# Attention kernel, one core: turning a group's blocks before scaling a context, and a later second copy of the values

## The reference

```python
q, k, v = (proj(Wq, bq), proj(Wk, bk), proj(Wv, bv))
scores = jnp.einsum('bhqd,bhkd->bhqk', q, k) * SCALE
mask = (adj_matrix + bond_matrix)[:, None, :, :]      # both are adj
scores = scores * mask
attn = jax.nn.softmax(scores, axis=-1)
ctx = jnp.einsum('bhqk,bhkd->bhqd', attn, v)
ctx = ctx.transpose(0, 2, 1, 3).reshape(b, seq_len, EMBED_DIM)
return jnp.einsum('bse,fe->bsf', ctx, Wo) + bo
```

## Time and profile before

| | |
|---|---|
| median of 3 runs | 418.44 us (414.08 to 418.67) |
| the profiled execution | 418.86 us, its span 416.3 us |
| mean granted clock of TensorE | 0.989 |
| PE busy | 92% |
| DVE busy | 93% |
| ACT busy | 87% |
| POOL busy | 60% |
| DMA | 222 GB/s on average |

### The profile page before, as it was taken

One profiled execution on the slowest core, in us unless ns is written; L12 is line 12 of the kernel. 1 busy time (PEld: TensorE's weight loads), 2 busy tenths in 40 slices (PEclk: granted clock), 3 DMA queues, 4 the chain that ended last, 5 costly groups with the idle time before them and its releaser, 6 DMA issues.

```text
span 416.3 us, 12182 instructions
## 1 busy us (share of the span) xinstructions
PE 382.1 (92%) x3628; PEld 291.4 (70%) x3628; DVE 386.2 (93%) x1592; ACT 361.6 (87%) x1223; POOL 249.6 (60%) x379
## 2 busy tenths in 40 slices
PE   8989999999996999999999999899999999997772
PEld 6766777777674877777777776677777777675542
DVE  4988999999997799999999999999999999999865
ACT  4699999989897798999999999889899999999560
POOL 3143557677573775748577575757758474555455
PEclk9999999999999899999999999999999999999898
DMA  8468889989988789889989888888999898888632
GB/s 272 131 173 238 236 201 254 245 237 247 244 237 234 191 223 244 244 243 251 253 237 246 241 237 235 230 242 233 248 245 248 227 232 208 219 234 183 144 105 76
DMA packets 65427, 92.29 MB, mean 222 GB/s; under 512 B 8529, under 2 KB 48722, under 8 KB 65362
## 3 DMA queue, kind: packets, MB, share of 16 engines
q1 hardware_dynamic: 47426, 66.35, 63.9%
q10 hardware_dynamic: 17936, 25.17, 18.0%
HBM read 26.22 MB, written 8.39 MB: 83 GB/s over the span
## 4 chain that ended last, share of the span: by engine, by line
DVE 33%; PE 28%; DMA 12%; SPq 11%; issue 9%; ACT 4%; POOL 1%; DVEq 0%; ACTq 0%; POOLq 0%
DVE boxes L540 15%; DVE probs L521 13%; SPq L208 9%; DMA v_boxed<-v 8%; PE ctx_bank L404 7%; PE out_bank L421 5%; PE proj_bank L333 5%; PE out_bank L351 4%; PE row_bank L264 3%; ACT probs L728 3%; DMA carried<-boxes 3%; PE turn_bank L281 2%; SPq L217 2%; DVE stats L567 1%; DVE low_top L530 1%
## 5 line engine op out<-in xcount | busy, mean ns | idle before, releaser
L728 ACT ACTIVATE probs<-probs,low_top 128x256 f32<-128x256 f32 x512 | 254.6, 504 | 12.1 <-DVE low_top L530 12.1
L521 DVE CUSTOM_DVE_ANT_0 probs<-row_bank,adj_rows 128x256 f32<-128x256 f32 x512 | 187.4, 414 | 6.7 <-PE row_bank L264 5.9
L540 DVE STREAM_TRANSPOSE boxes<-probs 128x1536 f32<-128x1536 f32 x62 | 109.6, 1768 | 0.0
L333 PE MATMUL proj_bank<-xt_parts,w_parts 128*128 128x512 f32 x360 | 99.2, 411 | 0.0
L728 ACT ACTIVATION_READ_ACCUMULATOR probs<-probs,low_top 128x1 f32 x512 | 99.1, 194 | 0.0
L333 PEld LDWEIGHTS proj_bank<-xt_parts,w_parts 128*128 128x128 f32 x360 | 62.9, 188 | 30.5 <-issue 19.9
L404 PE MATMUL ctx_bank<-carried,v_boxed 128*32 128x256 f32 x744 | 61.9, 392 | 18.3 <-DMA v_boxed<-v 12.2
L867 POOL COPY wide<-shares 128x512 f32<-128x512 f32 x32 | 19.5, 610 | 92.2 <-DVE shares L548 92.2
L264 PE MATMUL row_bank<-kq 32*128 32x256 f32 x1024 | 73.3, 400 | 0.5 <-DVE top L521 0.5
L404 PEld LDWEIGHTS ctx_bank<-carried,v_boxed 128*32 128x32 f32 x744 | 32.3, 111 | 43.4 <-issue 31.4
L264 PEld LDWEIGHTS row_bank<-kq 32*128 32x128 f32 x1024 | 46.3, 184 | 11.7 <-issue 6.4
(11 more groups left out here) (85 smaller groups left out, 461.1 us busy)
## 6 DMA issues: line engine op xcount, KB each, us to landing
carried<-boxes SPq DMA_DIRECT2D x248, 192.0 KB, 3.9
xt<-in_x_t SPq DMA_DIRECT2D x32, 256.0 KB, 3.5
adj_rows<-in_adj ACTq DMA_DIRECT2D x32, 256.0 KB, 4.8
xr<-in_x ACTq DMA_DIRECT2D x32, 256.0 KB, 3.8
v_boxed<-v SPq DMA_DIRECT2D x124, 64.0 KB, 3.0
out<-result ACTq DMA_DIRECT2D x31, 256.0 KB, 5.3
w_whole<-in_wk ACTq DMA_DIRECT2D x2, 128.0 KB, 3.7
w_whole<-in_wq SPq DMA_DIRECT2D x1, 256.0 KB, 4.3
```

What stands on the lines that cost most here:

```text
L333: last = nc.tensor.matmul(proj_bank[:], w_parts[:, a, which, t, c * P:(c + 1) * P], xt_parts[:, pair % 2, b, t, :], start=(half_ == 0 and ...
L521: last = nc.vector.tensor_tensor_reduce(probs[:, h % RING, t * S:(t + 1) * S], row_bank[j][:, t * S:(t + 1) * S], adj_rows[:, (g // 2) % 2 ...
L540: nc.vector.transpose(boxes[:, n % BOXES].rearrange("p a h (f q) -> p (h f) a q", q=D), probs[:, first:first + BOXED, :].rearrange("p h (f ...
L728: last = nc.scalar.activation(tile, tile, ACT.Exp, bias=low_top[:, g % 2, J * c + j, t:t + 1], accum_out=sums[:, g % 2, t, j * T + c:j * T ...
```

## The change

In DVE's `step(g)` the first box now stands ahead of `scale_context(g - 2)` and not behind it. In SP's `step(g)` `carry_v(g + 1)` now stands last, behind `carry_boxes(2g)`. Since the values' copies are now issued later, they are counted on four semaphores in place of two. Everything else, on all engines, stays as it was; no instruction is added or taken away.

```diff
-        stored, v_in = ([sem(f"{name}{n}") for n in range(2)] for name in ("stored", "v_in"))
-
-        x_in, adj_in, carried_in = ([sem(f"{name}{n}") for n in range(4)] for name in ("x_in", "adj_in", "carried_in"))
+        stored = [sem(f"stored{n}") for n in range(2)]
+
+        x_in, adj_in, v_in, carried_in = (
+            [sem(f"{name}{n}") for n in range(4)] for name in ("x_in", "adj_in", "v_in", "carried_in"))
...
-                                 ).then_inc(v_in[n % 2], 16)
+                                 ).then_inc(v_in[n % 4], 16)
...
                 if 0 < g <= LAST:
                     carry_boxes(2 * g - 1)
-                if 0 <= g + 1 < LAST:
-                    carry_v(g + 1)
                 if g > 0 and is_pair((g + 1) // 2 + 3):
                     load_x_t((g + 1) // 2 + 3, (g + 1) % 2)
                 if 0 <= g < LAST:
                     carry_boxes(2 * g)
+                if 0 <= g + 1 < LAST:
+                    carry_v(g + 1)
...
-                    pe.wait_ge(v_in[g % 2], 64 * (g // 2 + 1))
+                    pe.wait_ge(v_in[g % 4], 64 * (g // 4 + 1))
...
+                if is_group(2 * g - 1):
+                    box(2 * g - 1)
                 if 0 <= g - 2 < LAST:
                     scale_context(g - 2)
-                if is_group(2 * g - 1):
-                    box(2 * g - 1)
```

## The result

The changed kernel takes 436.0 us in the median of 6 runs (432.59 to 440.31), the kernel before 417.96 us (414.08 to 418.92): a ratio of 1.042, with a 95% interval of 1.036 to 1.049. It is slower, as forecast, and by about 18 us where 10 were forecast; the time lies on the upper edge of the range, 424 to 436. The profiled execution took 437.35 us with a span of 435.1 us, 18.8 more than before.

What follows compares the result with a forecast made beforehand. DVE's floor of 11.65 us and a two-step loop bound steps at 11.90; 26 steps at 12.33 plus 27.7 for two long ones gave +9.3, with +0.1 and +0.2 at the ends: 428.5 us, range 424 to 436.

Steps and rivals of the forecast that it cites:

- rival 2: SP's queue: SP becomes late with the first box's blocks, 0.8 us in 13 of 26 steps, about 438 us; chance 0.15.
- The chain from C to Y: DVE's context scaling over POOL and PE to the residual: 4.52 us, making DVE wait 0.69 per step, 12.33 a step.
- old two-step loop: First box, its DMAs, W, second half's rows, next but one first box: 0.25 us per step above DVE's floor, would go.
- first rival: The loop over two steps was all that mattered: steps fall to DVE's floor of 11.65 us, 410.5 us; chance 0.07.
- The two long steps: Steps of 16.19 and 13.49 us, each to shorten by about 1 us of new slack, taken as 27.7 together.
- third rival: The long steps were one-off: both fall to 12.33 us, giving 425.4 us, within 2%; chance 0.14.
- I take zero for the sum: SP's lateness with the first box's DMAs: counted as 0 us per step, with ends of 0 and +0.8.
- my best case: SP's issuing without a held issue: 2.7 us for the second box's DMAs, 2.7 for the copy; SP late by 0.
- my longest: SP's issuing with the second box's four DMAs at 4.76 us and the copy at 2.70; SP late by 2.1 us.
- the slack of 1.3: PE's room between the landing of the first box's blocks and O: 1.3 us of lateness absorbed.
- The ring order: DMA queue: the first box's blocks stand behind the values' 256 KB, landing at most 1.1 us later, inside the slack.

Runs made afterwards that it cites:

- e1: The kernel before with only DVE's part of the change, the first box ahead of the context's scaling; 425.98 us, 1.018.
- e5: The changed kernel with the values' copy issued behind the input's load and ahead of the second box's DMAs; 425.90 us, 1.022.
- e13: e1 with PE starting O on the high part and waiting for the low part only where a product reads it; 414.85 us, 0.992.
- e3: e1 with the second box also ahead of Y (add_residual) on DVE; 415.53 us, 0.998.
- e11: The changed kernel with two of the values' copy's four DMAs issued ahead of the second box's and two behind; 426.17 us, 1.019.
- e2: The kernel before with only SP's part of the change, the values' copy last in SP's step on four semaphores; 447.85 us, 1.070.
- e7: e2 with small filling matmuls on PE between the landings of the first box's four DMAs, ahead of W; 437.39 us, 1.047.
- e9: The kernel before with small filling matmuls on PE between the landings of the first box's DMAs, ahead of W; 419.74 us, 1.008.
- e8: e3 with small filling matmuls on PE between the landings of the first box's DMAs, ahead of W; 423.91 us, 1.018.
- e14: e3 with PE starting O on the high part and waiting for the low part only where it is read; 412.10 us, 0.985.

## Why the prediction was right, and where its size was off

The way, the chain behind it and the range were right; the size was not. 436.0 us is the very end of the range, which reached that far for the sake of rival 2, and it was rival 2's mechanism, on top of the forecast's, that brought the time there. That it lies on the edge and not beyond it is luck.

**The chain from C to Y: right, in kind and size.** The forecast 12.33 per step measured 12.28 in e1 and e5, with C at 1.70 behind the box (1.69 forecast) and 4.47 us from C to Y (4.52), both in the changed kernel's rows above. e13 shortened the chain and got its share back; e3 gave it room at Y and did the same.

**"The old two-step loop would cease to bind": right where SP is on time.** In e1 PE's waits ahead of W fell to 1.0 us. In the changed kernel they grew, to 22.7 us. The first rival (faster, since the old loop was all that mattered) failed by the chain that it left out: in e1 the old loop's waits are gone, and the time is 2% longer.

**The two long steps: off.** I carried 27.7 us for them; e1 has one step over 13.3 in place of two, and 344.9 us from the Y of step 2 to that of step 30 where the sum had 348.3. The sum was too low at the end: there the last two steps, behind the Y of step 30, take e1 1.9 us longer than before, where 0.2 was put down. The sum also didn't ask what makes a step long. In the step of 16.19 us, PE had waited 3.2 us ahead of W, and behind that wait its clock was at half (busy PE, PEld, DVE, ACT, POOL; clock; DMA share; GB/s):

```profile
134.10:137.50 3.40, 3.40 (x26) 2.42 (x18) 1.77 (x2) 0.73 (x2) 0.92 (x2) 0.50 0.83 232
```

So by these traces such a step isn't shortened by as much as the slack grows: in e1, where PE's wait is gone, it is gone too, and where waits come back it can come back. The changed kernel has one in mid-run, from the Y at 245.07 to that at 260.55:

```profile
245.07:260.55 15.48, 13.15 (x114) 9.96 (x113) 11.88 (x49) 11.29 (x39) 11.21 (x18) 0.89 0.85 222
```

It alone is 3.2 us longer than e1's step. The third rival, 425.4 us, is what DVE's part alone came to (425.98).

**SP: this is the step that failed.** "I take zero for the sum ... the second box's DMAs now have fewer DMAs just ahead of them, so a held issue should be rarer." The second box's issues are indeed held less, 3.1 us for four on average where it was 3.9. But the copy's four now take 3.8 us of issuing on average, not the 2.70 that I put down for them (2.8 on average before). Together that is 6.9 us, against 5.4 in my best case and 7.5 in my longest; SP was late by 1.6 us on average, and by more than the slack of 1.3 in 23 of 28 steps. That is the second rival's mechanism, at work all along and not in the longest cases only. The term that I put at zero measured 10.0 us, the difference between the changed kernel and e1. That this is just what the second rival was priced at is in part luck: 3.2 of the 9.9 us by which the 28 steps are longer than e1's come from the one step at the lower clock, which the rival's price, 0.8 us in half of the steps, doesn't have.

Why the copy's issues are held stays open. That they stand behind four DMAs of 192 KB isn't enough: in the kernel before they did too, right behind the first box's four,

```profile
210.92 2.99 SPq L208 DMA_DIRECT2D carried<-boxes  x4
```

and the copy's four followed at 214.01 in 2.70 us. The first of the four takes 0.6 us on average there and in e1, and 1.25 in the changed kernel, with four transfers of the queue still under way on average in each of the three. In the changed kernel, from 60 to 370 us, 49 of SP's 92 issues of over 0.9 us overlap an issue by ACT's queue, but only 27 of the 225 shorter ones; what ACT issues meanwhile may have a part in it, and no run separates that.

Over the whole run the two profiled executions differ by 18.8 us: 1.9 ahead of the first Y, 15.8 in the 28 steps, 1.1 behind them. The sum had 0.1, 9.3 and 0.2. Why the start is longer no run was made to show; e1 lost nothing there.

The loop over SP can be followed in the changed kernel's chain in order of time, from the second box at 207.92 (ends 209.69) through four DMAs, four DMAs and four DMAs to the landing and W:

```profile
209.72 0.54 SPq L209
...
212.84 1.60 SPq L218
214.48 0.82 SPq L218
215.34 0.59 SPq L218
215.98 0.59 SPq L218
216.67 0.57 SPq L209
...
218.62 4.79 DMA carried<-boxes
223.55 1.93 PE ctx_bank L405 x32
```

The first of the copy's DMAs is the held one, 1.60 us. No wait of SP for a box stands between 209.72 and 218.62; in this stretch SP's own issuing sets the pace.

**The ring order.** The rule that I drew on from the Trainium skill, "DMA: Bandwidth & Descriptors", section "Queues, rings and completion order", would have made the first box's blocks land later behind the copy's data. From the first issue to the last landing it is 6.6 us on average in the changed kernel (8.19 from the box's end, less 1.61 of lateness), 6.1 in e1 and 6.7 before. So by these averages the data of the copy cost 0.5 us against e1, and nothing against before, where the 1.1 us of the prediction was an estimate of the most; the larger price was SP's own time, 1.6 us.

**The two parts don't add.** DVE's part costs 9 us alone, SP's part 31 alone, both together 18. With the old order of DVE the two-step loop had no slack, so each lateness of SP went straight into the step, and behind the longer waits the clock fell; with the first box first there is slack of over a microsecond at W and O: e11's lateness of up to 1.3 us cost nothing. The same DMA order is worth 31, 10 or 6 us, by what DVE's order leaves it.

## What to carry to other kernels

When two neighbours on an engine change places, price both: here the one that went first gained 0.61 us, the one that went second lost 1.69, and the second had only 1.0 to spare. Find the length of the chain behind it where everybody is on time for it (often the last iteration), and compare it with what the engine does meanwhile. In a queue that only issues, look where it would be idle anyway: transfers that are needed late belong there, not last; and don't take the time of a held issue as gone because its neighbour moved. Here the second box's four became 0.7 us shorter, and the copy's four 1.0 us longer.

## What the runs showed that I had not expected

- A wait of PE of 2 us was followed by a stretch at 0.53 of the granted clock (e2), with W's first 18 matmuls at 2.12 in place of 1.27 us; e2's mean granted clock is 0.959 where the kernel before had 0.989. A lateness of SP of 0.7 us on average cost 31 us, a part of it in this way. Not every such wait was followed by a lower clock: behind e2's wait of 2.59 us at 282.5 it stayed full. Small matmuls in the wait brought some 10 us where the clock was falling (e7), and only cost where it wasn't (e9: +0.8%, e8: +8 us over e3).
- A small DMA's issue can be held as long as a large one's: in the changed kernel's chain the first 64 KB copy behind four 192 KB transfers took 1.60 us to issue, the following ones 0.6 to 0.8. In the kernel before, the same copy in a like place took 0.6.
- Starting a product on the half of its input that is ready first (e13, e14) was worth 11 us over e1 and 3.4 over e3 (2.5% and 1.3% by the ratios), for one wait that was moved.
